# Expert stage written out tile by tile, its bias added outside TensorE, weights loaded in pairs one after another, and half of the residual rows kept on chip

## The chip, the cores and the metric

The kernel runs on one core of one Trainium2 chip. The metric is the device time of one execution in microseconds (us). The core has five engines that each run their own instruction list: TensorE (PE, with its weight loads shown apart as PEld), VectorE (DVE), ScalarE (ACT), GpSimd (POOL) and SyncE (SP, which here only starts transfers). They meet through semaphores. Sixteen DMA engines move data between DRAM and the on-chip memory (SBUF).

## What is computed

One layer over 6250 rows of 256 numbers. A graph part sums weighted neighbour rows, runs a two-layer perceptron and a linear attention; its result is `x`. Then comes the part that the change touches, a mixture of 16 experts of which each row picks two:

```
gate_logits = x @ gate_w + gate_b                 # x here: layernorm of the layer's x
topk_vals, topk_idx = top_k(gate_logits, 2);  topk_w = softmax(topk_vals)
h          = relu(einsum('bsh,ehf->bsef', x, w1) + b1)       # 256 -> 512, per expert
expert_out = einsum('bsef,efh->bseh', h, w2) + b2            # 512 -> 256, per expert
moe = sum(topk_w[..., None] * take(expert_out, topk_idx), axis=2)
y   = x + moe
out = layer_x + layernorm(y) * gamma + beta
```

All of it is in 32-bit floats. The two weights `topk_w` of a row add up to one, so `x + sum(w * e)` is the same as `sum(w * (x + e))`.

## The kernel before, in words

The program is a chain of blocks; between two blocks all engines meet. Rows are handled in 49 tiles of 128.

1. Edges are sorted by row (0 to about 460 us).
2. The graph stage (about 460 to 1618 us): GpSimd gathers 858 sets of neighbour rows, TensorE sums them, and between these units the 49 tiles pass through perceptron, second layernorm and gate. ScalarE's `keep` (L1251 to L1261) stores a tile's normalised row `xn2` to DRAM, copies it into the SBUF array `xh`, and stores the residual row plus beta (`x2b`) to DRAM. Early in the stage VectorE splits the biases `b1` and `b2` (512 + 256 numbers for 16 experts) into three bf16 parts, `bias_split` (L1553 to L1565).
3. A short block (1618 to 1641 us) turns the choices into a list: XT = 114 tiles of up to 128 rows, each with one expert, experts in ascending order. It also starts the load of expert 0's weights.
4. The expert stage (1641 to 2165 us) works on one tile t after another, as a software pipeline. Each engine has a function `step`, run in a hardware loop of two tiles per round by `run_steps`:
   - GpSimd gathers the 128 rows of tile t+4 from DRAM into `tok` (2 buffers, L1884) and scatters the finished rows of tile t-1 to DRAM (L1876). Both read their row numbers from a one-column buffer that GpSimd fills by a copy first (L1864, L1870).
   - TensorE does the first products of tile t (`hidden sums`, 8 products of 128x128 that the profile counts as 16 halves, L1905), the turn of tile t+2 (2 transposes, L1915), then reads tile t-1's expert number into a register (L1919), adds the second bias by a bf16 product of `pick` and `bias_split` (L1923), and does the second products (4 products of 128x256, 8 halves, L1926).
   - ScalarE copies the tile's w1 block next to the others (L1943) after SyncE has counted the expert's weights as landed (`s_wready`, L1849), and copies the turned rows (L1949).
   - VectorE does bias and ReLU (4 instructions, L1962), builds `pick` (L1965) and copies the result to `yrow` (L1971).
   - SyncE has up to four experts' weights in flight (two loads of 512 KB each, L1719 and L1720).
5. The last stage (2166 to 2251 us): per tile TensorE mixes the two expert rows with their weights by diagonal matrices (L2025, L2026) on top of an identity product with `xh` that adds the normalised row (L2023). VectorE computes statistics (L2079, L2084), centres and scales (L2090), and adds the residual row (L2098). SyncE loads expert rows (256 KB per tile) and residual rows (128 KB per tile) and stores the output (128 KB per tile).

Sets of tiles in stage 5 are called groups: 18 of them, of 1 to 4 tiles.

## Time and profile before

| | us |
|---|---|
| median of 3 runs (2249.81 to 2251.22) | 2251.18 |
| the profiled execution, its own time | 2252.68 |
| its span, from first to last instruction | 2250.9 |
| PE busy over the span | 1678.2 (75%) |
| DVE busy | 1377.9 (61%) |
| POOL busy | 1328.5 (59%) |
| expert stage, first gather to last scatter begun | 1642.26 to 2162.66 |
| last stage, first load issued to last store issued | 2166.27 to 2246.65 |

The profile splits the span into instructions with start, duration, and the idle time before each with what ended it. In the rows below a source line (L1905) is a line of the kernel before; `x16` merges consecutive instructions; `[0.68 <-DMA ...]` says that the engine sat idle for 0.68 us until that transfer landed; `<-issue` is idle time in which the engine's own instruction list was late. [...] PEldq is TensorE's own instruction reader.

### The profile page before, as it was taken

The numbers are of one execution on the slowest core, as the hardware profiler recorded it, in microseconds if no ns is written. First come the engines' busy times: TensorE is split into PE (matmuls) and PEld (weight loads), VectorE is DVE, ScalarE is ACT, GpSimd is POOL, SyncE is SP. The second block draws the span as 40 slices with busy tenths as digits, with TensorE's granted clock in tenths as the row PEclk, the third lists the DMA queues.
The fourth block names the chain that finished last, engine by engine and source line by source line (L and its number), as shares of the span: only waits on it lengthen the run. The fifth ranks groups of instructions, "written<-read, shape, count | busy, mean of one in ns | idle before, by whom it ended". The sixth has DMA issues, their size and how long they took to land. (4 is left out here: it accounts for less than half of the span.)

```text
span 2250.9 us, 40865 instructions
## 1 busy us (share of the span) xinstructions
PE 1678.2 (75%) x9702; PEld 1414.8 (63%) x9703; DVE 1377.9 (61%) x4034; ACT 764.5 (34%) x2288; POOL 1328.5 (59%) x1455
## 2 busy tenths in 40 slices
PE   6007888237777787888777887776569999999987
PEld 4007877236655666676666665555458888888876
DVE  4999888368776666666666666564433444334348
ACT  5718889100001323323323222221223333333333
POOL 0007888378777777777777777776024555555510
PEclk9558999668878999889999889997789999999999
DMA  5001011354434444444444444448373111111257
GB/s 162 0 0 36 20 36 36 4 164 131 123 105 121 131 127 126 133 127 127 132 127 126 130 122 126 119 126 91 55 262 104 61 62 59 61 61 61 59 201 279
DMA packets 133895, 232.71 MB, mean 103 GB/s; under 512 B 28854, under 2 KB 85784, under 8 KB 133767
## 3 DMA queue, kind: packets, MB, share of 16 engines
q0 software_dynamic: 56096, 144.39, 23.6%
q1 hardware_dynamic: 49975, 60.99, 8.6%
q10 hardware_dynamic: 27696, 25.83, 3.6%
q8 instruction: 55, 0.90, 0.2%
q14 instruction: 73, 0.60, 0.1%
HBM read 188.69 MB, written 42.43 MB: 103 GB/s over the span
## 5 line engine op out<-in xcount | busy, mean ns | idle before, releaser
L1309 POOL DMA_INDIRECT lower<-xn_rows,lower x858 | 851.1, 992 | 270.1 <-issue 234.6
L1334 PE MATMUL bank<-lower 128*128 x960 | 351.0, 451 | 216.4 <-SPq L1183 175.1
L1334 PEld LDWEIGHTS bank<-lower 128*128 128x128 f32 x960 | 172.9, 213 | 300.7 <-issue 290.1
L1472 DVE TENSOR_TENSOR xh<-xh,bank 128x256 f32 x480 | 200.0, 417 | 242.6 <-PE bank L1335 240.9
L1455 DVE TENSOR_SCALAR lower<-iota_n,lower 128x128 f32<-128x128 f32 x960 | 295.4, 361 | 76.0 <-issue 54.5
L606 POOL DMA_INDIRECT edge_records_sorted<-lower x112 | 204.7, 1828 | 209.0 <-ACT lower L755 179.7
L1335 PE MATMUL bank<-lower 128*128 x960 | 322.9, 421 | 0.0
L683 PE MATMUL bank<-lower 128*64 128x128 f32 x1568 | 192.0, 287 | 113.2 <-ACT lower L739 108.8
L683 PEld LDWEIGHTS bank<-lower 128*64 128x64 f32 x1568 | 185.8, 146 | 116.9 <-DVE lower L942 109.4
L1876 POOL DMA_INDIRECT expert_rows<-arena,dest_idx x114 | 114.6, 1005 | 215.4 <-DVE arena L1971 202.9
L1962 DVE TENSOR_SCALAR arena<-bank,b_tile 128x128 f32<-128x128 f32 x456 | 128.3, 344 | 173.5 <-PE bank L1905 173.5
L1335 PEld LDWEIGHTS bank<-lower 128*128 128x128 f32 x960 | 207.2, 216 | 36.8
L1905 PEld LDWEIGHTS bank<-arena 128*128 128x128 f32 x1824 | 224.1, 194 | 9.0 <-issue 3.0
L1926 PE MATMUL bank<-upper,arena 128*128 x912 | 229.0, 395 | 0.0
L1905 PE MATMUL bank<-arena 128*128 128x128 f32 x1824 | 224.6, 277 | 2.6 <-ACT arena L1943 2.6
L1926 PEld LDWEIGHTS bank<-upper,arena 128*128 128x128 f32 x912 | 167.4, 193 | 30.8 <-issue 5.1
L739 ACT ACTIVATE lower<-lower 128x32 f32<-128x32 f32 x784 | 169.3, 309 | 7.4 <-DVE lower L927 6.6
L1250 ACT ACTIVATE std<-mv,eps_col 128x1 f32<-128x1 f32 x49 | 14.4, 295 | 420.8 <-DVE mv L1622 420.8
L1943 ACT ACTIVATE arena<-lower 128x1024 f32 x114 | 120.5, 1057 | 66.6 <-issue 57.8
L1971 DVE COPY arena<-bank 128x256 f32<-128x256 f32 x114 | 48.4, 425 | 150.1 <-PE bank L1926 150.1
L1949 ACT ACTIVATE arena<-bank 128x256 f32<-128x256 f32 x114 | 43.8, 384 | 284.2 <-PE bank L1915 284.2
L1884 POOL DMA_INDIRECT arena<-xn_rows,tok_idx x114 | 109.4, 960 | 40.1 <-issue 32.5
(337 smaller groups left out, 2531.0 us busy)
## 6 DMA issues: line engine op xcount, KB each, us to landing
lower<-xn_rows,lower POOLq DMA_INDIRECT x858
lower<-in_L_ffn_w SPq DMA_DIRECT2D x16, 512.0 KB, 9.0
upper<-in_L_ffn_w SPq DMA_DIRECT2D x16, 512.0 KB, 10.5
xn_rows<-xh SPq DMA_DIRECT2D x7, 896.0 KB, 4.2
lower<-xn_rows ACTq DMA_DIRECT2D x49, 128.0 KB
xn_rows<-lower ACTq DMA_DIRECT2D x49, 128.0 KB
x_plus_beta<-lower ACTq DMA_DIRECT2D x49, 128.0 KB
upper<-in_x SPq DMA_DIRECT2D x1, 6144.0 KB
```

Source lines behind the costliest of these rows:

```text
L606: pool.indirect_dma_start(rec_dram, bass.IndirectOffsetOnAxis(quad_idx[i][:, c:c + 1], 0), quads[i][:, c * QW:(c + 1) * QW], None).then_in ...
L683: mm = pe.matmul(bank[6 + p][0:NQ * QW, 0:P], moving[p][:, e].rearrange("p c w -> p (c w)"), row_hot[p][:, e, :], start=e == 0, stop=e == ...
L739: done = act.activation(moving[p][:, e, :, 1], col_hot[p][:, e, :], ACT.Copy, scale=group_wgt[p][:, e:e + 1])
L1309: pool.indirect_dma_start(edge_rows[:, t % ROUND, :], None, xn_dram, bass.IndirectOffsetOnAxis(source.bitcast(U32)[:, t:t + 1], 0)).then_i ...
L1334: pe.matmul(sums_at(u), edge_sel[:, 2 * u % ESEL, :], rows_flat[:, ds(at, D)], start=True, stop=False)
L1335: pe.matmul(sums_at(u), edge_sel[:, (2 * u + 1) % ESEL, :], rows_flat[:, ds(at + D, D)], start=False, stop=True).then_inc(s_sum, 1)
L1455: dve.tensor_scalar(edge_sel[:, (2 * u + h) % ESEL, :], iota_n[:], lane[:, at:at + 1], weight_s[:, at:at + 1], ALU.is_equal, ALU.mult).the ...
L1472: dve.tensor_tensor(xh[:, at], xh[:, at], sums_at(u), ALU.add).then_inc(s_acc, 1)
L1905: mm = pe.matmul(bank[2 + p][:, m * P:(m + 1) * P], w1_tile[p][:, c * F + m * P:c * F + (m + 1) * P], tokT[p][:, c * P:(c + 1) * P], start ...
L1926: mm = pe.matmul(bank[6 + p][:, 0:D], hidT[p][:, m * P:(m + 1) * P], upper[:, ds(e * (FC * D) + m * D, D)], start=False, stop=m == FC - 1)
L1943: act.activation(w1_tile[p], lower[:, ds(e * (DC * F), DC * F)], ACT.Copy).then_inc(s_w1t, 1)
L1962: dve.tensor_scalar(hidT[p][:, m * P:(m + 1) * P], bank[2 + p][:, m * P:(m + 1) * P], b1_tile[:, ds(t + m * XT, 1)], 0.0, ALU.add, ALU.max ...
```

## The change

- **Bias.** `b2` is loaded once in plain form to all 128 partitions (`b2_all`, 2 MB, in block 3). VectorE adds gathered row and `b2` of the tile's expert into `yrow` (`biased`, three tiles ahead), and later adds TensorE's result to it (`finish`). So an expert row carries the normalised row too, and the product L1923, its `pick` and the identity product L2023 go. `bias_split` shrinks from 768 to 512 columns.
- **Order.** TensorE, VectorE and GpSimd have the 114 tiles written out one by one; ScalarE keeps its loop. Row numbers are used from `rows_idx` and `dest_idx` directly, without GpSimd copies. `tok` has 4 buffers, `yrow` 6; gathers run 6 tiles ahead.
- **Weights.** From expert 1 on, each 512 KB load waits until the one before has landed; the first waits for the third gather.
- **Residual rows.** `xh` now receives `x2b` instead of `xn2`; the last stage takes the first KEEP = 25 tiles from there and loads only the other 24. The rest of `xh` holds `b2_all` and `yrow`.

TensorE, expert stage, one tile before (`bank` is PSUM, `arena` holds rows, turned rows, hidden rows and the w1 copy, `upper` the w2 weights; names in brackets are the semaphores waited on):

```order
L1905 MATMUL bank<-arena 128x128 [waits expert_hidden,tile_w1_copied,rows_transpose_copied]
L1905 MATMUL bank<-arena 128x128 x7
L1915 MATMUL bank<-ident,arena 128x128 [waits rows_transpose_copied,rows_landed1]
L1915 MATMUL bank<-ident,arena 128x128
L1919 TENSOR_LOAD expert_row
L1919 ISA x2
L1923 MATMUL bank<-bias_split,arena 128x256 [waits expert_rows,bias_pick]
L1926 ISA [waits expert_hidden]
L1926 MATMUL bank<-upper,arena 128x256
L1926 ISA
L1926 MATMUL bank<-upper,arena 128x256
```

and the same tile after:

```order
L1893 MATMUL bank<-arena 128x128 [waits expert_hidden,tile_w1_copied,rows_transpose_copied]
L1893 MATMUL bank<-arena 128x128 x7
L1903 MATMUL bank<-ident,arena 128x128 [waits rows_transpose_copied,rows_landed1]
L1903 MATMUL bank<-ident,arena 128x128
L1912 ISA [waits expert_hidden,expert_rows]
L1912 MATMUL bank<-upper,arena 128x256
L1912 ISA
L1912 MATMUL bank<-upper,arena 128x256
L1880 TENSOR_LOAD expert_row
L1912 ISA
L1912 MATMUL bank<-upper,arena 128x256
```

The register load has moved from behind the turn of the rows to the middle of the second products, for the next tile, and the bias product is gone.

GpSimd, start of the expert stage, before (`row_index_staged` and `result_index_staged` are its own copies of row numbers):

```order
L1870 CAST tok_idx<-rows_all 128x1 [waits rows_landed0]
L1884 DMA arena<-xn_rows,tok_idx 128x256 [waits row_index_staged0,rows_transposed]
L1864 CAST dest_idx<-arena 128x1
L1870 CAST tok_idx<-rows_all 128x1 [waits rows_landed1]
L1876 DMA expert_rows<-arena,dest_idx 27137x256 [waits result_index_staged0,expert_rows]
L1884 DMA arena<-xn_rows,tok_idx 128x256 [waits row_index_staged1,rows_transposed]
```

and after:

```order
L1858 DMA arena<-xn_rows,rows_idx 128x256 x4
L1858 DMA arena<-xn_rows,rows_idx 128x256 [waits rows_transposed,rows_with_bias] x3
L1864 DMA expert_rows<-xh,dest_idx 27137x256 [waits expert_rows]
L1858 DMA arena<-xn_rows,rows_idx 128x256 [waits rows_transposed,rows_with_bias]
L1864 DMA expert_rows<-xh,dest_idx 27137x256 [waits expert_rows]
```

Four gathers go out at once and seven stand ahead of the first scatter.

SyncE, expert weights, before:

```order
L1719 DMA lower<-in_L_ffn_w 128x2x512 [waits weights_of_expert0,rows_landed1]
L1720 DMA upper<-in_L_ffn_w 128x4x256
L1719 DMA lower<-in_L_ffn_w 128x2x512
L1720 DMA upper<-in_L_ffn_w 128x4x256
L1719 DMA lower<-in_L_ffn_w 128x2x512
```

and after:

```order
L1845 DMA lower<-in_L_ffn_w 128x2x512 [waits expert_weights_loaded,rows_landed2]
L1847 DMA upper<-in_L_ffn_w 128x4x256 [waits expert_weights_loaded]
L1845 DMA lower<-in_L_ffn_w 128x2x512 [waits expert_weights_loaded]
L1847 DMA upper<-in_L_ffn_w 128x4x256 [waits expert_weights_loaded]
L1845 DMA lower<-in_L_ffn_w 128x2x512 [waits expert_weights_loaded]
```

Every load now stands behind the landing of the one before it.

The diff, cut to its core:

```diff
-        bias_f = xn_rows[0:96, 0:F + D]
+        bias_f = xn_rows[0:96, 0:F]
...
+        TOKB, YB = 4, 6
+        KEEP = 25
+        carve = carver(xh[:, KEEP * D:NT * D], (NT - KEEP) * D)
+        b2_all = carve(NX * D)
+        yrow = [carve(D) for _ in range(YB)]
...
                     at = ds(bucket_now[s] * D, D)
-                    act.activation(xh[:, at], xn2[s % XB], ACT.Copy).then_inc(s_xn2k, 1)
                     act.dma_start(xn2_dram[ds(bucket_now[s] * P, P), :], xn2[s % XB]).then_inc(s_xn2st, 16)
                     act.wait_ge(s_x2b, s + 1)
                     act.dma_start(x2b_dram[:, at], x2b).then_inc(s_x2st, 16)
+                    act.activation(xh[:, at], x2b, ACT.Copy).then_inc(s_x2k, 1)
...
                 sp.dma_start(gamma_row, row(gamma)).then_inc(s_gamma, 16)
+                sp.dma_start(b2_all, row(b2.rearrange("e d -> (e d)"))).then_inc(s_b2, 16)
...
+                sp.wait_ge(s_we, 32)
+                sp.sem_inc(s_wready, 1)
+                sp.wait_ge(s_tok[2], 16)
+                for e in range(1, NX):
+                    sp.dma_start(w1_sb[:, e], w1[e].rearrange("(c p) f -> p c f", p=P)).then_inc(s_we, 16)
+                    sp.wait_ge(s_we, 32 * e + 16)
+                    sp.dma_start(w2_sb[:, e], w2[e].rearrange("(m p) d -> p m d", p=P)).then_inc(s_we, 16)
+                    sp.wait_ge(s_we, 32 * e + 32)
                     sp.sem_inc(s_wready, 1)
...
+                def gather(t):
+                    if t >= TOKB:
+                        pool.wait_ge(s_tT, t - TOKB + 1)
+                        pool.wait_ge(s_yb, t - TOKB + 1)
+                    pool.indirect_dma_start(tok[t % TOKB], None, xn2_dram, ...rows_idx[:, t:t + 1]...)
+                def scatter(t):
+                    pool.wait_ge(s_yr, t + 1)
+                    pool.indirect_dma_start(y_dram, ...dest_idx[:, t:t + 1]..., yrow[t % YB], None)
+                for t in range(-AHEAD, XT):
+                    if t + AHEAD < XT:
+                        gather(t + AHEAD)
+                    if t >= 0:
+                        scatter(t)
...
+                for t in range(-2, XT + 1):          # TensorE
+                    if 0 <= t < XT:
+                        hidden(t)
+                    if t + 2 < XT:
+                        turn(t + 2)
+                    if t >= 1:
+                        second(t - 1)
...
+                def biased(t):                       # VectorE
+                    e = dve.value_load(expert_row[0:1, t:t + 1], min_val=0, max_val=NX - 1)
+                    dve.wait_ge(s_tok[t % TOKB], t // TOKB * 16 + 16)
+                    if t >= YB:
+                        dve.wait_ge(s_yst[t % YB], t // YB * 16)
+                    dve.tensor_tensor(yrow[t % YB], tok[t % TOKB], b2_all[:, ds(e * D, D)], ALU.add).then_inc(s_yb, 1)
+                def finish(t):
+                    dve.wait_ge(s_y, t + 1)
+                    dve.wait_ge(s_yb, t + 1)
+                    dve.tensor_tensor(yrow[t % YB], yrow[t % YB], bank[6 + t % 2][:, 0:D], ALU.add).then_inc(s_yr, 1)
...
-                        pe.matmul(mixed, ident[:], xh[:, t * D:(t + 1) * D], start=True, stop=False)
                         pe.wait_ge(s_fdiag, TOPK * (t + 1))
-                        pe.matmul(mixed, diag[t % NDG * TOPK], first_row(t), start=False, stop=False)
+                        pe.matmul(mixed, diag[t % NDG * TOPK], first_row(t), start=True, stop=False)
...
+                    if i in OFF:                     # groups from tile 25 on
+                        x2_of = x2_rows[o % XBUF]
+                    else:
+                        x2_of = xh[:, t0 * D:(t0 + m) * D]
```

## Rows read from the trace of the kernel before

**Rows 1.** Busy time by stretch of the expert stage: PE, PEld, DVE, ACT, POOL, clock, DMA
```profile
1645.00:1700.00 55.00, 40.06 (x212) 34.59 (x213) 12.82 (x46) 14.10 (x20) 17.97 (x33) 0.81 0.94 324
1700.00:2155.00 455.00, 430.87 (x2832) 382.09 (x2831) 181.70 (x629) 149.86 (x208) 235.84 (x414) 1.00 0.19 60
```

**Rows 2.** Timeline of two tiles 13 us apart, TensorE: start, us, instruction, idle before
```profile
2101.30 1.95 PE L1905 MATMUL bank<-arena 128*128 128x128 f32 x16
2103.08 0.38 PE L1915 MATMUL bank<-ident,arena 128*128 128x128 f32 x2
2103.30 0.27 PE L1923 MATMUL bank<-bias_split,arena 96*128 96x256 bf16 x1
2103.41 1.89 PE L1926 MATMUL bank<-upper,arena 128*128 x8
...
2105.14 1.95 PE L1905 MATMUL bank<-arena 128*128 128x128 f32 x16
...
2114.58 1.95 PE L1905 MATMUL bank<-arena 128*128 128x128 f32 x16
...
2117.13 0.44 PE L1915 MATMUL bank<-ident,arena 128*128 128x128 f32 x2 [0.60 <-DMA arena<-xn_rows,tok_idx]
...
2117.95 0.28 PE L1923 MATMUL bank<-bias_split,arena 96*128 96x256 bf16 x1 [0.39 <-issue]
...
2120.00 1.95 PE L1905 MATMUL bank<-arena 128*128 128x128 f32 x16
```

**Rows 3.** Waits from 1700 to 2150: us in total, times, longest
```profile
PEld bank L1923 <- issue: 31.2, 61, 0.6
```

**Rows 4.** TensorE's register load (L1919): ns min/median/max, first and last start
```profile
L1919 PEldq TENSOR_LOAD <-expert_row x114: 297/302/320, 1656.7 to 2156.6; - x114
```

**Rows 5.** Timeline, start of the expert stage
```profile
1642.26 0.97 POOL L1884 DMA_INDIRECT arena<-xn_rows,tok_idx  x1 [0.82 <-POOL tok_idx L1870]
...
1645.17 0.66 PE L1915 MATMUL bank<-ident,arena 128*128 128x128 f32 x2 [7.69 <-DMA arena<-xn_rows,tok_idx]
...
1653.68 1.06 ACT L1943 ACTIVATE arena<-lower 128x1024 f32 x1 [4.84 <-SPq L1849]
...
1657.31 1.06 ACT L1943 ACTIVATE arena<-lower 128x1024 f32 x1 [2.29 <-SPq L1849]
...
1660.47 1.95 PE L1905 MATMUL bank<-arena 128*128 128x128 f32 x16
```

**Rows 6.** Time from issue to landing: w1 and w2 of expert 0, alone; then all w1
```profile
DMA to landing us min/median/max: 4.4/4.4/4.4
...
DMA to landing us min/median/max: 3.8/3.8/3.8
...
lower<-in_L_ffn_w SPq DMA_DIRECT2D x16, 512.0 KB, 9.0
```

**Rows 7.** VectorE's bias and ReLU: busy us, mean ns, idle before
```profile
L1962 DVE TENSOR_SCALAR arena<-bank,b_tile 128x128 f32<-128x128 f32 x456 | 128.3, 344 | 173.5 <-PE bank L1905 173.5
```

**Rows 8.** Timeline, end of the expert stage
```profile
2155.63 1.95 PE L1905 MATMUL bank<-arena 128*128 128x128 f32 x16
...
2162.66 0.98 POOL L1876 DMA_INDIRECT expert_rows<-arena,dest_idx  x1 [0.82 <-POOL dest_idx L1864]
```

**Rows 9.** Last stage: a stretch by engine (columns as Rows 1), waits as Rows 3
```profile
2191.31:2230.32 39.01, 38.71 (x171) 31.55 (x170) 36.34 (x124) 20.57 (x63) 0.00 (x0) 1.00 1.00 371
...
DVE stats L2079 <- PE bank L2026: 18.6, 16, 10.5
```

**Rows 10.** Timeline, last stage
```profile
2172.18 0.43 DVE L2079 BATCH_NORM_STATS2 stats<-bank 128x6 f32<-128x256 f32 x1 [10.46 <-PE bank L2026]
...
2191.31 0.41 DVE L2084 BATCH_NORM_AGGREGATE mv<-stats 128x2 f32<-128x6 f32 x3
...
2200.98 0.41 DVE L2084 BATCH_NORM_AGGREGATE mv<-stats 128x2 f32<-128x6 f32 x3
```

**Rows 11.** VectorE's bias split in the graph stage (L1556), columns as Rows 4
```profile
L1556 DVE CAST bias_split<-arena x6: 541/550/551, 487.0 to 494.6; 32x768 bf16<-32x768 f32 x6
```

More of the change, by code:

```diff
@@ L360, in gps_layer @@
         hidT = [carve(F) for _ in range(2)]
-        yrow = [carve(D) for _ in range(2)]
-        pick = [carve(P // 2).bitcast(BF16)[0:96, :] for _ in range(2)]
         dest_all = carve(XT)
@@ L1699, in _ @@
                         unit(u)
[L1704 removed]
+        s_we = sem("expert_weights_loaded")
         s_gap = sem("gate_gaps")
@@ new lines, in turn, with second @@
+                def turn(t):
+                    pe.wait_ge(s_tok[t % TOKB], t // TOKB * 16 + 16)
+                    if t >= 2:
+                        pe.wait_ge(s_tTe, t - 1)
+                    for c in range(DC):
+                        mm = pe.transpose(bank[t % 2][:, c * P:(c + 1) * P], tok[t % TOKB][:, c * P:(c + 1) * P], ident[:])
+                    mm.then_inc(s_tT, 1)
+                def second(t):
+                    p = t % 2
+                    if t >= 2:
+                        pe.wait_ge(s_yr, t - 1)
+                    pe.wait_ge(s_hr, t * FC + FC)
+                    for m in range(FC):
+                        mm = pe.matmul(bank[6 + p][:, 0:D], hidT[p][:, m * P:(m + 1) * P],
+                                       upper[:, ds(expert[t] * (FC * D) + m * D, D)], start=m == 0, stop=m == FC - 1)
+                        if m == 1 and t + 1 < XT:
+                            load_expert(t + 1)
+                    mm.then_inc(s_y, 1)
@@ L1973, in _, with hidden @@
-                run_steps(dve, step, *E_STEPS)
+                LETB = 3
+                def hidden(t):
+                    p = t % 2
+                    dve.wait_ge(s_h, t + 1)
+                    if t >= 2:
+                        dve.wait_ge(s_y, t - 1)
+                    for m in range(FC):
+                        dve.tensor_scalar(hidT[p][:, m * P:(m + 1) * P], bank[2 + p][:, m * P:(m + 1) * P],
+                                          b1_tile[:, t + m * XT:t + m * XT + 1], 0.0, ALU.add, ALU.max).then_inc(s_hr, 1)
@@ L1977, in gps_layer @@
+                dve.wait_ge(s_b2, 16)
+                for t in range(-LETB, XT + 1):
+                    if 0 <= t < XT:
+                        hidden(t)
+                    if t + LETB < XT:
+                        biased(t + LETB)
+                    if t >= 1:
+                        finish(t - 1)
         ENDS = {0: ((0, 1), (1, 1), (2, 2), (4, 3)), NG - 1: ((0, 3), (3, 2), (5, 1), (6, 1))}
```

201 lines of the change are left out of this document (66 added, 135 removed).

## The prediction

> **What bounds the kernel now.** I read the profile from the whole to the part: first the busy shares in 40 slices, then busy time by stretch for the two stages that the change touches, then the timeline of a few tiles, then the waits. [...] One tile takes 3.84 us (2101.30 to 2105.14), another close by 5.42 (2114.58 to 2120.00), with the same instructions [rows 2]. The first is TensorE's own pace: 1.78 for the 16 halves of the first products, 0.22 for the turn, 0.11 for the bias product, 1.73 for the second products. The second is the same with a wait for the gathered rows, and behind it 0.82 between the turn (2117.13) and the bias product (2117.95) instead of 0.22. The gap is the register load of 0.30 us [rows 4], with its register work, that stands behind the turn in TensorE's list: where the rows are early, the reader is ahead of the array and the load costs nothing; where they come just in time, the reader has been held at the turn and the load is exposed. It is exposed at 61 of the some 100 tiles between 1700 and 2150 [rows 3]. From the third tile's first products (1660.47) to the last tile's (2155.63) are 495.16 us for 111 tiles [rows 5, 8]: 4.46 each, 0.62 above the pace. So the stage is bound by late rows and by the weights' start, not by arithmetic.
>
> In its first 55 us the clock averages 0.81 and DMA is 94% busy with weights [rows 1]; the row gathers queue behind them, and only 8 tiles are done (212 matmuls at 27 a tile).
>
> In the last stage TensorE is busy 38.71 of 39.01 us, VectorE 36.34, and DMA is full [rows 9]. Seven tiles take 9.67 us (2191.31 to 2200.98) [rows 10]. VectorE waits for TensorE 16 times for 18.6 us, 10.5 of that before the first tile [rows 9]: TensorE is the bound, with VectorE close behind.
>
> **The change part by part**, counted in the profiled execution (2252.68 us, span 2250.9; the median of the runs is 1.5 below it).
>
> *Pace of a tile.* The bias product goes: 3.84 - 0.11 = 3.73 us. The rows: a gather now stands six tiles ahead of the scatter of its step, and four buffers let it go as soon as the tile four before it has been turned and biased. Its data is needed about three and a half tiles, 13 us, after its issue. A gather in the loaded first stretch would have to take more than that to be late. The load of the expert number now stands between the second and third of four products, for the tile after. The reader has 0.43 us of array work per product in front of it and is no longer held at the turn, so I take its cost as nothing; if the cover fails it is between the load's 0.30 [rows 4] and the whole gap's 0.60 (0.82 - 0.22) [rows 2] on each tile, 33 to 67 us in all. ScalarE's copies and loop stay; it is busy 150 of 455 us [rows 1]. GpSimd drops its two copies and keeps two issues of about 1 us. VectorE has four ReLUs of 0.34 us, loses the pick, gains one add and turns its copy into another; for an add of twice their width I take 0.45, a bit above [rows 7]: 2.3 us, and 2.6 with a register load that nothing covers, under 3.73. `finish` stands behind `biased` in VectorE's list, and the scatter behind `finish`; the row that `biased` waits for was gathered three tiles before. 111 x 3.73 = 414.0. I add 2 for a stretch at 1.2 GHz when the third tile begins after an idle TensorE, and 4 for stray waits: 420.0 against 495.16, **-75.2**. Ends: 414 (no stray, -81) and 4.33 a tile (3.73 + 0.60, 481, -14).
>
> *Start of the stage.* The reference's own gate on the given inputs, counted, gives tiles per expert 1, 1, 41, 1, 18, 14, 1, 0, 2, 1, 1, 4, 12, 0, 8, and the spare tiles last. So tile 1 needs expert 1 and tile 2 expert 2; the trace agrees: ScalarE's copies at 1653.68 and 1657.31 waited for weights [rows 5]. After the change expert 2 is behind four loads in series. The first gather starts at about 1641.25 instead of 1642.26, since the copy and its 0.82 wait are gone [rows 5]; the third begins 2.5 later (two issues of 0.97 and the gaps) and lands 2.9 after that, as the first did (1642.26 to 1645.17), 1646.7. A load on its own took 4.4 and 3.8 us [rows 6], so expert 2 is there at 1646.7 + 2 x 8.2 = 1663.1, and with the copy of 1.06 the third tile starts at 1664.4 instead of 1660.47: **+3.9**. Lower end: the loads take 3.8 each, +2; upper end: they take the 9.0 of loads that share the queues [rows 6], +23. Expert 3 is first needed at tile 43, some 150 us later, and all fifteen pairs take 123 us, so nothing waits after that. The 2 MB of `b2_all` go in ahead of expert 0's w1 at 1618, in a block in which DMA is idle; at the 371 GB/s of [rows 9] it is 6 us, and w1 has 23 until the stage begins: no cost.
>
> *End of the stage.* The last scatter loses GpSimd's copy and the wait of 0.82 for it [rows 8]; with the copy's own 0.2: **-1.0**.
>
> *Last stage.* The identity product is a third of TensorE's work: six halves at 0.216 (1.73 / 8 in [rows 2]) are 1.29 us a tile, four are 0.86. VectorE is next: 9.67 us for seven tiles less its waits in them (0.6) is 9.07, 1.30 a tile. The 8.1 us of waits after the first tile go. The first tile comes 0.9 earlier, two halves at half the clock [rows 9, 10]. Against it, the first tiles at 1.2 GHz need 4 x 0.43 = 1.7 us each on TensorE, more than VectorE's 1.3: I give back 1.5. **-7.5.** The traffic falls from 49 x 512 KB by 25 x 128 KB, 25.7 to 22.4 MB, so DMA, full now, does not take TensorE's place. Ends: -9 (all waits go), and +10 if TensorE stays at half its clock throughout: 49 x 1.71 = 84 us against the 74.5 from the first statistics at 2172.18 [rows 10] to the last store.
>
> [...]
>
> *Graph stage.* The bias split runs from 487.0 to 495.2 on VectorE (the last cast at 494.6 and its 0.55), each step waiting for the one before, 8.2 us [rows 11]. Its width falls to two thirds: 0 to -2.7. VectorE is what holds the heads behind it, and the gathers are not yet at their own pace there, so I take **-2.0**. The copy into `xh` has the same size and only changes place in ScalarE's list; VectorE's new wait for it comes a whole tile later: nothing.
>
> Sum: -75.2 + 3.9 - 1.0 - 7.5 - 2.0 = -81.8. From 2252.68 that is 2170.9, and at the level of the median **2169.5 us**.
>
> **Rivals.**
> 1. *The register load stays exposed*, or rows are still only just in time: about 0.4 a tile, 111 x 0.4 = 44, less the 4 of stray: 2210. For it: 61 exposed loads. Against: in the tile at 2101.30 the same load cost nothing, 3.84. 8%.
> 2. *Serial weights land as slowly as shared ones*, 9.0 each instead of 4.1: third tile at 1683 to 1686, +19 to +23: about 2190. For it: gathers and scatters still share the queues. Against: the solo loads of [rows 6]. 6%.
> 3. *The last stage loses its clock*, as above: up to +17.5 on my sum, 2187; half of that, 2178, is likelier. 10%.
> 4. *Slower than before: the clock of the expert stage.* If TensorE is granted the mean 0.81 of the first stretch [rows 1] through the stage, a tile takes 3.73 / 0.81 = 4.60 and 111 take 511: +16 + 3.9 - 1.0 - 7.5 - 2.0 = +9, 2260. It decides from a mean clock under 0.84. For it: 0.81 with a TensorE that is held up. Against: 1.00 over the 455 us behind it, with more gaps than there will be. 3%.
>
> **How the numbers follow.** My forecast has 73%, with its own range 2162 to 2178. What a measurement of this kernel can tell from no change is about 0.2%, 4.5 us. Every case but the last is faster by more. The fourth holds the chance of slower, and 2% lie in between, where rivals 1 and 2 would meet: faster 0.95, same 0.02, slower 0.03. For eight in ten the range takes in rivals 2 and 3 and leaves out the first: 2160 to 2190.
>
> **What would show it.** Right: first products of consecutive tiles 3.73 apart, no idle time at the turn, third tile at about 1662 (1664.4 less the graph stage's 2), copy waits on weights at tiles 1 and 2 only, DMA share about 0.4 for 130 us, last stage paced by VectorE at 9.1 us for seven tiles. Wrong: tiles that alternate as before; a clock under 0.95 in the last stage; an idle gap between second and third of the second products; ScalarE waiting for weights beyond tile 2.

## The result and the profile after

| | before | after |
|---|---|---|
| median of 4 runs | 2250.49 us (2248.23 to 2251.22) | 2163.53 us (2162.59 to 2167.23) |
| ratio, 95% interval | | 0.9618 [0.9602, 0.9635] |
| profiled execution, span | 2252.68, 2250.9 us | 2162.62, 2160.9 us |
| mean granted clock (1.00 is full speed) | 0.886 | 0.884 |

The forecast was 2169.5 us, in a range of 2160 to 2190; the time is 6.0 below the forecast. The span went down by 90.0 us, the medians by 87.0. The two spans divide at four places that both timelines have; "tile 2" is the third tile, counted from 0:

| stretch | before | after | difference | predicted |
|---|---|---|---|---|
| start to the end of the sort (first gather of the graph stage) | 449.3 | 446.3 | -3.0 | 0 |
| from there to the first gather of the expert stage | 1193.0 | 1191.6 | -1.4 | -3.0 |
| first gather to tile 2's first products | 18.2 | 21.9 | +3.7 | +4.9 |
| 111 tiles, tile 2 to the last | 495.2 | 414.1 | -81.1 | -75.2 |
| last tile to the last stage's first load | 10.6 | 11.6 | +1.0 | -1.0 |
| last stage, first load to the end | 84.6 | 75.4 | -9.2 | -7.5 |

The predicted +4.9 is the +3.9 of the text with the 1.0 by which the first gather was to come earlier; that 1.0 stands in the row above it, with the graph stage's -2.0. The first row is no effect of the change: in the kernels below that ran at the same speed, the sort ended at 448.0 to 454.6.

The busy time by stretch of the changed kernel's expert stage (columns as in [rows 1]: PE, PEld, DVE, ACT, POOL, granted clock, DMA share, GB/s):

```profile
1645.00:1700.00 55.00, 48.49 (x321) 45.45 (x321) 23.02 (x75) 18.39 (x26) 21.92 (x24) 0.90 0.60 188
1700.00:2080.00 380.00, 379.27 (x2636) 357.73 (x2634) 190.48 (x608) 143.65 (x199) 194.33 (x199) 1.00 0.30 92
```

Read it against [rows 1]: in the first 55 us 321 matmuls instead of 212 (301 when the window is laid at the same distance behind the first gather, which came 4.4 us earlier here), with DMA 60% busy and not 94; behind it TensorE has 0.7 us idle in 380, where it had 24 in 455. The timeline of TensorE there, and the time of the register load:

```profile
1700.92 1.95 PE L1893 MATMUL bank<-arena 128*128 128x128 f32 x16
1702.71 0.38 PE L1903 MATMUL bank<-ident,arena 128*128 128x128 f32 x2
1702.93 1.89 PE L1912 MATMUL bank<-upper,arena 128*128 x8
1704.65 1.95 PE L1893 MATMUL bank<-arena 128*128 128x128 f32 x16
...
1708.39 1.95 PE L1893 MATMUL bank<-arena 128*128 128x128 f32 x16
```
```profile
L1880 PEldq TENSOR_LOAD <-expert_row x114: 295/301/714, 1637.2 to 2074.1; - x114
```

1700.92, 1704.65, 1708.39: 3.73 us each, and the rows of one tile follow each other with no idle time in brackets. This is the first of the two tiles of [rows 2] less its bias product, all the way to the end. The load (0.30 us, as in [rows 4]) is done 114 times and shows nowhere as idle time.

The start of the stage, for POOL, ScalarE, SyncE and TensorE (columns as in [rows 5]):

```profile
1637.89 0.95 POOL L1858 DMA_INDIRECT arena<-xn_rows,rows_idx  x1 [23.15 <-POOLq L1718]
...
1650.84 1.06 ACT L1939 ACTIVATE arena<-lower 128x1024 f32 x1 [7.04 <-SPq L1849]
...
1658.64 1.06 ACT L1939 ACTIVATE arena<-lower 128x1024 f32 x1 [6.47 <-SPq L1849]
```
```profile
1643.06 0.37 SPq L1845 DMA_DIRECT2D lower<-in_L_ffn_w  x1
1646.77 0.37 SPq L1847 DMA_DIRECT2D upper<-in_L_ffn_w  x1
1650.78 0.37 SPq L1845 DMA_DIRECT2D lower<-in_L_ffn_w  x1
1654.63 0.37 SPq L1847 DMA_DIRECT2D upper<-in_L_ffn_w  x1
1658.58 0.37 SPq L1845 DMA_DIRECT2D lower<-in_L_ffn_w  x1
```
```profile
1643.51 3.75 PE L1893 MATMUL bank<-arena 128*128 128x128 f32 x16
...
1652.04 3.65 PE L1893 MATMUL bank<-arena 128*128 128x128 f32 x16 [4.35 <-ACT arena L1939]
...
1659.80 2.02 PE L1893 MATMUL bank<-arena 128*128 128x128 f32 x16 [2.16 <-issue]
```

Each load is issued when the one before it has landed, 3.7 to 4.0 us apart; ScalarE's two copies start at the very end of the second and the fourth of them (1650.84, 1658.64), and TensorE starts tiles 1 and 2 behind those copies. Only three other copies wait for weights, by 0.4 to 0.7 us each, and no product waits for them.

The end of the stage, before and after: GpSimd's drain, the instruction with which it closes the stage behind its last scatter.

```profile
L1844 POOLq DRAIN  x1: 706/706/706, 2165.3 to 2165.3; - x1
```
```profile
2073.87 1.95 PE L1893 MATMUL bank<-arena 128*128 128x128 f32 x16
...
2080.55 0.95 POOL L1864 DMA_INDIRECT expert_rows<-xh,dest_idx  x1 [0.77 <-DVE xh L1972]
```
```profile
L1838 POOLq DRAIN  x1: 2009/2009/2009, 2083.2 to 2083.2; - x1
```

The last scatter stands 6.68 us behind the last tile's first products instead of 7.03, but the drain behind it takes 2009 ns where it took 706.

The last stage, 40 us of it, then VectorE's only waits of note in the stage, then seven tiles of it:

```profile
2100.90:2140.90 40.00, 29.58 (x126) 22.83 (x125) 39.68 (x139) 23.26 (x71) 0.00 (x0) 1.00 1.01 368
```
```profile
DVE stats L2087 <- PE bank L2035: 12.1, 4, 10.7
```
```profile
2110.15 1.24 DVE L2098 SCALAR_TENSOR_TENSOR upper<-bank,mv,arena 128x256 f32<-128x256 f32 x3
...
2119.03 1.24 DVE L2098 SCALAR_TENSOR_TENSOR upper<-bank,mv,arena 128x256 f32<-128x256 f32 x3
```

Against [rows 9]: TensorE is busy 29.6 of 40 us instead of 38.7 of 39, VectorE 39.7 instead of 36.3, the clock still 1.00. Of the 18.6 us that VectorE waited for TensorE, only the 10.7 before the first tile are left with 1.4 behind them. Seven tiles take 8.88 us (2110.15 to 2119.03), where they took 9.67.

### The profile page after: what moved, and what is told of

It reads as the page before. It is cut to its first block and busy times, and to the rows that moved or that the text cites. A ratio compares the mean times of both kernels' runs of the same rounds, so it can differ in the third digit from the quotient of the medians.

```text
span 2160.9 us, 38464 instructions
## 1 busy us (share of the span) xinstructions
PE 1603.4 (74%) x9490; PEld 1379.4 (64%) x9490; DVE 1391.8 (64%) x4033; ACT 768.0 (36%) x2288; POOL 1286.3 (60%) x1227
## 5 line engine op out<-in xcount | busy, mean ns | idle before, releaser
L1864 POOL DMA_INDIRECT expert_rows<-xh,dest_idx x114 | 112.1, 983 | 183.4 <-DVE xh L1972 169.1
L1912 PE MATMUL bank<-upper,arena 128*128 x912 | 215.6, 379 | 0.0
L1858 POOL DMA_INDIRECT arena<-xn_rows,rows_idx x114 | 110.7, 971 | 60.5 <-issue 33.5
L941 DVE TENSOR_TENSOR lower<-upper,iota_n 128x3584 f32<-128x3584 f32 (+1 forms) x28 | 108.7, 3883 | 0.0
```

The lines of the kernel that those rows point to most:

```text
L1912: mm = pe.matmul(bank[6 + p][:, 0:D], hidT[p][:, m * P:(m + 1) * P], upper[:, ds(expert[t] * (FC * D) + m * D, D)], start=m == 0, stop=m = ...
```

## The experiments

Twelve kernels ran, in three groups of four, e1 to e4, e5 to e8 and e9 to e12, each on one chip. The chips of the first and of the third group are slower, nearly all of it in one place, in each of the eight kernels profiled there: from the sort to the first gather of the expert stage they take 1409 to 1431 us, where the others take 1192 to 1198 (last section); the sort itself ends 1 to 22 us later. Before was not profiled on these chips; its runs there take 2478 to 2502 us. Each ratio is against before on the same chip. The expert stage is read from its first gather to the last tile's first products, "G" below, and the last stage from its first load to the end, "L". Both hold over the chips: the changed kernel has G 436.0 and L 75.4 in its first profile and 437.6 and 75.7 on such a chip (e12). Before: G 513.4, L 84.6.

| kernel | G us | tile 2 behind first gather | steady median a tile | L us | ratio to before |
|---|---|---|---|---|---|
| before | 513.4 | 18.2 | 4.27 | 84.6 | 1 |
| changed | 436.0 | 21.9 | 3.73 | 75.4 | 0.9618 |
| e1 weights abreast | 433.8 | 17.9 | 3.73 | 76.2 | 0.9649 |
| e2 two row buffers | 687.9 | 21.1 | 5.79 | 75.8 | 1.0630 |
| e3 load behind turn | 436.9 | 21.8 | 3.73 | 75.9 | 0.9653 |
| e4 both | 693.8 | 21.6 | 5.78 | 76.2 | 1.0658 |
| e5 before, paced | 517.5 | 21.8 | 4.30 | 84.3 | 1.0001 |
| e6 two buffers, add last | 476.6 | 21.8 | 3.88 | 75.3 | 0.9802 |
| e7 four buffers, near | 688.5 | 22.1 | 5.79 | 75.5 | 1.0709 |
| e8 wide bias split | 436.1 | 22.1 | 3.73 | 75.5 | 0.9605 |
| e9 all rows loaded | 437.4 | 21.8 | 3.73 | 78.2 | 0.9670 |
| e10 rows and identity | 437.3 | 21.7 | 3.73 | 84.5 | 0.9702 |
| e11 weights early | 429.9 | 14.2 | 3.73 | 76.2 | 0.9601 |
| e12 changed again | 437.6 | 21.9 | 3.73 | 75.7 | 0.9660 |

The theory at the start was the prediction's: the stage was bound by rows that came late, because of the weights in the queues at first and two row buffers throughout, with a register load exposed behind them. The rivals: the load's place in the list, and the order of GpSimd's and VectorE's lists.

**e1: the weights four experts abreast again**

```diff
...
+                for e in range(1, WAHEAD):
+                    load_weights(e)
+                load_weights(WAHEAD)
                 for e in range(1, NX):
-                    sp.dma_start(w1_sb[:, e], ...).then_inc(s_we, 16)
-                    sp.wait_ge(s_we, 32 * e + 16)
-                    sp.dma_start(w2_sb[:, e], ...).then_inc(s_we, 16)
-                    sp.wait_ge(s_we, 32 * e + 32)
+                    sp.wait_ge(s_wr[e % WAHEAD], ...)
                     sp.sem_inc(s_wready, 1)
+                    if e + WAHEAD < NX:
+                        load_weights(e + WAHEAD)
```

> The changed kernel, but the weights of the experts again in groups of four in flight, as before the change. Pacing theory (as in the prediction: the start of the stage is set by what shares the queues with the first gathers): experts 1 to 4 then land together, some 35 us after the third gather; each of the eight loads takes 9 us or more, the clock of the first 55 us falls from 0.90 to about 0.8, expert 2 is there no earlier than in the changed kernel, and the four-row lookahead keeps the gathers early all the same: third tile within 3 us of 1659.8, pace behind 1700 unchanged at 3.73, stage 3 to 25 us longer, 2166 to 2188. Rival (the lookahead alone does everything; pacing delays expert 2 and is worth nothing or less): third tile 1 to 4 us earlier and the same pace: 2159 to 2163.

Measured: ratio 0.9649 [0.9626, 0.9672], beside e3 (the changed kernel with one thing changed that cost nothing) at 0.9653 on the same chip. Tile 2 starts 17.9 us behind the first gather and not 21.9, the pace is 3.73, G is 433.8. The first products of the first three tiles:

```profile
1888.28 3.75 PE L1899 MATMUL bank<-arena 128*128 128x128 f32 x16
...
1895.17 2.66 PE L1899 MATMUL bank<-arena 128*128 128x128 f32 x16 [2.71 <-ACT arena L1945]
...
1900.64 1.95 PE L1899 MATMUL bank<-arena 128*128 128x128 f32 x16
```

The rival was right. With the rows asked for three tiles ahead of the bias add it does not matter that DMA is 98% busy with weights in the 55 us from 1890: from tile 2's first products to tile 8's it takes 22.4 us, where it took 39.5 before. VectorE's bias add does wait there, 11.8 us in all, for earlier scatters to land, but nothing of it reaches TensorE. In the trace pacing the weights costs 2 to 4 us in this kernel and brings nothing; the two ratios do not resolve so little.

**e2: two row buffers, gathers four tiles ahead**

```diff
-        TOKB, YB = 4, 6
+        TOKB, YB = 2, 6
...
-        AHEAD = 6
+        AHEAD = 4
...
-                sp.wait_ge(s_tok[2], 16)
+                sp.wait_ge(s_tok[1], 16)
```

> The changed kernel with two row buffers and four tiles ahead, as before the change (SP's weights start behind the second gather instead of the third). A gather now waits until the tile two before it has been turned and biased. Theory A (the prediction's: the rows of before came late because of the two buffers and their place in the queue): rows are again just in time on part of the tiles, waits on DMA at the turn, 0.2 to 0.6 a tile, 2185 to 2230. Theory B (a row gather lands in 2.6 to 4.6 us and two buffers leave some 7 us, so what mattered was that GpSimd no longer stands behind copies and scatters): pace stays 3.73, 2161 to 2168.

Measured: 1.063 [1.061, 1.0651], slower than before itself, and outside both theories. It takes 5.79 us a tile. One round of it in the trace, without the weight loads and SyncE:

```profile
2099.69 0.98 POOL L1864 DMA_INDIRECT expert_rows<-xh,dest_idx  x1 [3.56 <-DVE xh L1972]
...
2100.98 0.96 POOL L1858 DMA_INDIRECT arena<-xn_rows,rows_idx  x1 [0.31 <-issue]
2103.82 0.20 PEld L1903 LDWEIGHTS bank<-ident,arena 128*128 128x128 f32 x2 [2.03 <-DMA arena<-xn_rows,rows_idx]
...
2103.92 0.42 DVE L1967 TENSOR_TENSOR xh<-arena,xh 128x256 f32<-128x256 f32 x1 [4.03 <-DMA arena<-xn_rows,rows_idx]
...
2104.26 0.41 DVE L1972 TENSOR_TENSOR xh<-xh,bank 128x256 f32<-128x256 f32 x1
...
2105.52 0.98 POOL L1864 DMA_INDIRECT expert_rows<-xh,dest_idx  x1 [3.57 <-DVE xh L1972]
```

One follows from the other, by the releaser that a row names or by its place in the list of its engine: the scatter (0.98, and a gap of 0.31), the gather from 2100.98 to its landing at 2103.92, the bias add L1967 that waited 4.03 us for it, the last add L1972 that stands behind it in VectorE's list, and the scatter, whose issue begins 0.85 behind the end of that. Round to round it is 5.83 us. The ring closes because `biased(t + 3)` waits for rows whose gather stands behind the scatter that `finish`, queued behind `biased`, has to release. That gave a theory with two tests, e6 and e7.

**e3 and e4: the register load behind the turn, with early rows and with late ones**

```diff
                 def second(t):
                     p = t % 2
+                    load_expert(t)
                     ...
-                        if m == 1 and t + 1 < XT:
-                            load_expert(t + 1)
```

> The changed kernel, only with the register load of the expert number taken from between the second products of the tile before and put behind the turn, where it was before the change; the rows stay early. Theory A (the prediction's: the load is exposed only where TensorE's reader is held up at the turn by late rows): with early rows it costs nothing, pace 3.73, 2162 to 2167. Theory B (the load's place is what matters; it is exposed on any tile behind the turn): 0.3 to 0.6 a tile on all 111, 33 to 67 us, 2196 to 2230.

Measured: 0.9653 [0.9629, 0.9676], G 436.9, pace 3.73. Theory A: with early rows the load costs nothing in its old place either. Moving it was not needed. In e4 this edit and that of e2 are made together.

> Two row buffers with four tiles ahead, and the register load behind the turn: both of the last two at once. If late rows and the load's place only cost together (theory A of both), the pace goes back to about 4.2 to 4.4 a tile with waits on DMA at the turn and a gap behind it, 2215 to 2240, more than the two single costs added. If they are independent, the cost is the sum of the two single ones.

Measured: 1.0658 [1.0633, 1.0683], G 693.8 against 687.9 in e2. With late rows the load does show, as in [rows 3]; the first row is e4's from 1950 to 2500, the second a tile of it:

```profile
PEld bank L1913 <- issue: 32.5, 91, 0.4
```
```profile
2105.78 1.59 PEld L1913 LDWEIGHTS bank<-upper,arena 128*128 128x128 f32 x8 [0.36 <-issue]
```

0.36 us at 91 of the tiles, and yet the steady pace is 5.78 as in e2: TensorE is not in the ring, so idle time in front of it costs nothing there. I had expected a pace of 4.2 to 4.4 and the two to cost clearly more together than added. Neither came: G grows by 252 in e2, by 1 in e3 and by 258 in e4, one profile each, and the intervals of e2 and e4 overlap, so the 5 between are not settled.

**e5: before, with paced weights**

```diff
...
+                for e in range(1, NX):
+                    sp.dma_start(w1_sb[:, e], ...).then_inc(s_we[0], 16)
+                    sp.wait_ge(s_we[0], 32 * e + 16)
+                    sp.dma_start(w2_sb[:, e], ...).then_inc(s_we[0], 16)
+                    sp.wait_ge(s_we[0], 32 * e + 32)
                     sp.sem_inc(s_wready, 1)
-                    if e == 0:
-                        sp.wait_ge(s_tok[1], 16)
-                        for later in range(1, WAHEAD):
-                            load_weights(sp, later)
-                    if e + WAHEAD < NX:
-                        load_weights(sp, e + WAHEAD)
```

> The kernel before the change, only with the experts' weights loaded one transfer at a time, as in the changed kernel. With the lookahead of the changed kernel pacing the weights cost 3.9 us at the third tile and gave nothing back. Theory A (before the change the late rows of the first 55 us were late because of the weights in the queues, the prediction's reading): here pacing gives back part of the first stretch, 8 tiles in 55 us become 10 to 12, 10 to 20 us faster over the stage, less 4 at the third tile. Theory B (the rows are late by the order of GpSimd's list, whatever else is in the queues): the pace stays at 4.4 to 4.5 a tile from the first tiles on, and the kernel is the same or up to 4 us slower.

Measured: 1.0001 [0.9987, 1.0016]. This kernel's first gather is at 1649.42, 7.2 us behind that of before, so the stretch to lay beside the first of [rows 1] is the one at the same distance from it:

```profile
1652.16:1707.16 55.00, 44.77 (x263) 39.33 (x264) 16.23 (x58) 16.74 (x24) 22.22 (x41) 0.87 0.55 171
```

That is 263 matmuls and not 212, some ten tiles and not eight. The time from issue to landing of a row gather says why; before from 1640 to 1700, before from 1700 on, and e5 from 1649 to 1707:

```profile
DMA to landing us min/median/max: 2.8/5.6/6.2
```
```profile
DMA to landing us min/median/max: 2.7/2.8/3.6
```
```profile
DMA to landing us min/median/max: 2.7/3.1/3.6
```

With four experts' weights in flight a gather took up to 6.2 us, and from tile 2 to tile 8 it was 39.5 us; paced, a gather took at most 3.6 in this stretch, and the six tiles 27.0. So theory A was right on what made the rows late in the first 55 us. It was wrong on the whole: tile 2 comes 3.6 us later, and the 8.9 us that e5 is ahead at tile 8 are gone by tile 24 (127.3 us behind the first gather, before 126.0). The paced weights are still being loaded until some 120 us, where before has issued its last load at 47, and in that time two of e5's tiles take 7.5 and 7.6 us. The 111 tiles take 495.7 us, against 495.2. Theory B has the rest: behind tile 24 both kernels need some 4.4 us a tile, before with no weights left to load. What holds the rows there is not the weights, and e5 doesn't show what it is.

**e6: two buffers, but the last add ahead of the bias add**

```diff
...
+                    if t >= 1:
+                        finish(t - 1)
                     if t + LETB < XT:
                         biased(t + LETB)
-                    if t >= 1:
-                        finish(t - 1)
```

The edit of e2 is in it too.

> Two row buffers and four tiles ahead, as in the kernel that took 5.8 us a tile, but in VectorE's list the last add of a tile stands ahead of the bias add that waits for a later tile's rows. Ring theory (from the trace of that kernel: gather issue and landing 3.9, bias add and last add 0.8, scatter issue and gap 1.3 follow each other round and round, because the bias add of tile t+3 waits for rows that are gathered behind the scatter of tile t-1, which waits for the add behind it): the ring is broken, pace 3.73 to 3.9. Rival (two buffers are too few in themselves, since a gather waits for the turn and the bias add of the tile two before): pace between 4.5 and 5.8.

Measured: 0.9802 [0.9769, 0.9836]. From e2's 5.8 the pace falls to a median of 3.88, on average 4.10 (454.8 us for 111 tiles): the ring is broken by the order of two instructions, as the ring theory said, though the average is 0.2 above its range. What is left from 1700 to 2100:

```profile
PEld bank L1903 <- DMA arena<-xn_rows,rows_idx: 22.9, 37, 2.5
```

Over the 111 tiles e6 is 40.7 us above the changed kernel, and the row above gives 22.9 of it as TensorE's waits for rows. That is the price of two buffers with four tiles ahead; the two were not parted in this order of the adds.

**e7: four buffers, but gathers only four tiles ahead**

```diff
-        AHEAD = 6
+        AHEAD = 4
```

> Four row buffers as in the changed kernel, but gathers only four tiles ahead of the scatter of their step instead of six; VectorE's list as in the changed kernel. Ring theory: the rows of tile t+4 are issued behind the scatter of tile t-1 and the bias add of tile t+4 stands in front of the last add of tile t, so the ring is there with any number of buffers: 5.6 to 5.8 a tile. Rival (the buffers are what counts): 3.73 a tile.

Measured: 1.0709 [1.0674, 1.0743], G 688.5, the same as e2 with half the buffers. From 1700 to 2300:

```profile
DVE xh L1967 <- DMA arena<-xn_rows,rows_idx: 420.8, 100, 6.5
...
POOL expert_rows L1864 <- DVE xh L1972: 353.5, 95, 5.2
```

VectorE waits 4.2 us for rows at each of 100 tiles, and GpSimd 3.7 for VectorE. In this order of VectorE's list four buffers are worth nothing without the two tiles more of lookahead.

**e8: the bias split at its old width**

```diff
-        bias_f = xn_rows[0:96, 0:F]
-        bias_r = xn_rows[0:96, F:2 * F]
+        bias_f = xn_rows[0:96, 0:F + D]
+        bias_r = xn_rows[0:96, F + D:2 * (F + D)]
...
```

> The changed kernel with the bias split of the graph stage at its old width of 768 instead of 512 columns (the extra 256 are loaded and split, and not used). If the narrower split is what brought 1.8 us on VectorE there: the split takes 8.2 us again (6.45 in the changed kernel). By the prediction 2.0 of it reach the end of the graph stage. Rival: they are lost in the wait of the heads for gathered rows, and nothing before the expert stage moves by more than runs of one kernel differ.

Measured: 0.9605 [0.9573, 0.9637]. The split takes 8.5 us (489.97 to 498.45) and 6.5 in the changed kernel. From the sort's end to the first gather: 1196.2, beside 1194.6 and 1195.3 in e6 and e7, which have the narrow split and ran on the same chip. e5, with the wide split of before and on the same chip too, takes 1198.3, of which 1.0 may be its later first gather. So 1 to 3 us of the split may reach the end of the graph stage, but these are single profiles, and those of one width differ by 0.7 and 1.1 themselves; it stays inconclusive.

**e9 and e10: the last stage's loads, and the identity product**

```diff
-        OFF = [i for i, (t0, _, _) in enumerate(GROUPS) if t0 >= KEEP]
+        OFF = list(range(len(GROUPS)))
```
```diff
+                        pe.matmul(mixed, ident[:], xh[:, t * D:(t + 1) * D], start=True, stop=True)
                         pe.wait_ge(s_fdiag, TOPK * (t + 1))
```

The first edit is in both, the second in e10 only.

> The changed kernel, but in the last stage the residual rows of all 49 tiles are loaded again from DRAM instead of 24; no identity product. It is the last stage that is asked: from SyncE's first load there to the end were 84.6 us before and 75.4 in the changed kernel. Theory A (the prediction's: TensorE was the bound and the identity product's end is the gain): the stage stays within 1.5 us of 75.4, since the 25.7 MB of before need 69 us at the 371 GB/s that it reached. Rival (DMA was full before, and the 3.3 MB less are the gain): 82 to 85 us.

> As the one before (all residual rows loaded again), and with the identity product back on TensorE as extra work: its result is overwritten by the next product, so the output doesn't use it. Theory A: this brings the old last stage back, 83 to 86 us, with VectorE waiting for TensorE 15 to 19 us in its steady part. Rival (TensorE was not the bound, the loads are): same as the one before.

Measured: L 78.2 in e9 (ratio 0.9670 [0.9638, 0.9701]) and 84.5 in e10 (0.9702 [0.9661, 0.9743]); 75.7 in e12 on the same chip, 84.6 before. e10 first, then e9, 40 us of the stage each:

```profile
2344.10:2384.10 40.00, 39.35 (x174) 31.93 (x172) 36.98 (x125) 21.08 (x65) 0.00 (x0) 1.00 1.00 370
```
```profile
2348.50:2388.50 40.00, 30.02 (x126) 22.57 (x124) 39.68 (x139) 23.21 (x71) 0.00 (x0) 1.00 1.06 403
```

e10 is the last stage of before again: 84.5 us against 84.6, with TensorE as full as in [rows 9]. With the identity product gone (e9) VectorE is the bound, and DMA moves 403 GB/s where it moved 370: it had looked full at a share of 1.00 and was not. VectorE's waits in the stage, e10 and then e9:

```profile
DVE stats L2090 <- PE bank L2036: 20.0, 16, 11.6
```
```profile
DVE upper L2113 <- DMA lower<-x_plus_beta: 1.3, 1, 1.3
```

Behind the first tile VectorE waits 8.4 us for TensorE in e10 (20.0 less 11.6), as the 8.1 of [rows 9], and not the 15 to 19 that the expectation gave. Of the 9 us the identity product is 6.3 (84.5 to 78.2) and the 25 row tiles kept in SBUF are 2.5 (78.2 to 75.7): mostly theory A, with a part for the loads that it put at under 1.5. That part lies at the start and not in the steady run: e9 issues its fourth store 21.2 us behind the first load, where e12 does at 18.8, and from there to the end they take the same time. A wait of VectorE for residual rows, 1.3, is half of it.

**e11 and e12: the weights of experts 1 to 3 in the idle block before, and the changed kernel again**

```diff
                 sp.dma_start(w2_sb[:, 0], ...).then_inc(s_we, 16)
+                for e in range(1, WAHEAD):
+                    sp.dma_start(w1_sb[:, e], ...).then_inc(s_we, 16)
+                    sp.wait_ge(s_lists, TOPK * FC * (e + 1))
+                    sp.dma_start(w2_sb[:, e], ...).then_inc(s_we, 16)
...
-                sp.wait_ge(s_we, 32)
-                sp.sem_inc(s_wready, 1)
-                sp.wait_ge(s_tok[2], 16)
-                for e in range(1, NX):
+                sp.wait_ge(s_we, 32 * WAHEAD)
+                sp.sem_inc(s_wready, WAHEAD)
+                for e in range(WAHEAD, NX):
```

> The changed kernel, with the weights of experts 1 to 3 loaded in the block before the expert stage, in which DMA is nearly idle; experts 4 to 15 stay one at a time. In the changed kernel tiles 1 and 2 start 14.1 and 21.9 us behind the first gather because they wait for weights, and tile 0 at 5.6. Theory A (only weights hold those two tiles): tile 1 at about 9.4, tile 2 at 13 to 14.5, all after it 3.73 apart: 7 to 9 us off the whole, ratio to before about 0.958 where the changed kernel has 0.962. [...]

> The changed kernel itself once more, unaltered, on the chip of the three before, to read them against: stages as in its first profile (tile 2 at 21.9 us behind the first gather, 3.73 a tile, last stage 75.4), ratio 0.960 to 0.9635; the graph stage may differ with the chip.

Measured, on one chip: e11 2386.33 us median (6 runs), ratio 0.9601 [0.9571, 0.9631]; e12 2398.01 (6 runs), 0.9660 [0.9631, 0.9689]. The first gather of e11 is at 1865.21; its first three tiles:

```profile
1871.70 3.75 PE L1896 MATMUL bank<-arena 128*128 128x128 f32 x16 [0.52 <-issue]
...
1875.67 1.97 PE L1896 MATMUL bank<-arena 128*128 128x128 f32 x16
...
1879.42 1.95 PE L1896 MATMUL bank<-arena 128*128 128x128 f32 x16
```

Tile 2 is at 14.2 us and not at 21.9, G is 429.9 and not 437.6: both 7.7 less, theory A (tile 1 comes at 10.5, where it gave 9.4). The first products of tile 0 take 3.75 us at a granted clock of 0.50 (1871.7 to 1875.4), those of tile 1 1.97 at 0.99 (1875.67 to 1877.6). Whole runs give 11.7 between the medians with intervals that just touch, so I trust the 7.7 of the trace. This kernel beats before by 4%, and the changed one by those 7.7 us. e12 has the stages of the first profile, but its ratio of 0.9660 lies above the 0.960 to 0.9635 expected: the 88 us less are a smaller share of the 2486 us that before takes on this chip.

## Why the prediction came out right, step by step

- *What bounds the stage.* "Bound by late rows and by the weights' start, not by arithmetic" held. So did the reason that the text gave for late rows in the first 55 us, "the row gathers queue behind" the weights: their landing took up to 6.2 us there and 2.8 behind it, and e5, which thins the weights out, has at most 3.6 and gets from tile 2 to tile 8 in 27.0 us and not 39.5. What did not hold is the cure: paced weights alone win nothing (e5), and with rows asked for early no pacing is needed (e1).
- *Pace of a tile.* 3.73 was exact (1700.92, 1704.65, 1708.39). 111 tiles took 414.1 us, the lower end of the text; the +2 for the clock and +4 for stray waits were not needed. The runs give the clock as a share of full speed alone, so the 1.2 GHz that the text names with this +2 is shown by none of them. What they show is tile 1's first products at 3.65 us and a granted clock of 0.53 (1652.0 to 1655.7), and tile 2's, after 2.16 us of idle TensorE, at 2.02 and 1.00, with tile 3 following 3.81 behind (1663.61). That the load costs nothing was right. Its new place between the products, by which the text argued, was not what did it: it costs nothing behind the turn too, once the rows are early (e3), as the text had said of the tiles of before with early rows.
- *The sum.* The span fell by 90.0 and not 81.8. Of the 8.2 between, 5.9 are the stray waits and 3.0 are the sort, which the change doesn't touch and which was luck; the start and the last stage gave 1.2 and 1.7 more than forecast, the graph stage and the end 1.6 and 2.0 less. The total is closer than its parts because they partly cancel.
- *What it rests on.* The text took four buffers and six tiles ahead as one step, and wrote of the wait in `biased` only that its row "was gathered three tiles before". That is the condition on which the whole edit hangs, and that six tiles ahead met it was not worked out, so it was in part luck. With four tiles ahead, one tile before, the kernel is 7% slower than before instead of 4% faster (e7), and no rival named it: rival 4 looked for a slower kernel in the clock. The price could be read from the change: 2.9 from a gather's issue to its landing [rows 5], two adds of 0.45 by the text's own estimate and a scatter of 1.0 [rows 8] are 4.8 a tile before any gap, against 3.73.
- *How the 81.1 us divide.* The bias product is 111 x 0.11 = 12.2. Four buffers with six tiles ahead instead of two with four are 40.7 (e6). The last 28.2 us, between before's 495.2 and e6's 454.8 less the bias product, are GpSimd's two copies, the load exposed behind late rows (31.2 us in [rows 3]), the slow gathers of the first 55 us and the new order together; I didn't run them apart. By place, 17.0 of the 81.1 lie in the six tiles from tile 2 to tile 8 (39.5 and 22.5).
- *Start.* Four loads in series took 15.5 us (1643.06 to 1658.58), predicted 16.4. With the sort 3.0 earlier than in the profile of before, 1664.4 - 2.0 - 3.0 = 1659.4 for tile 2; it came at 1659.80. That it is so close is chance: the first gather came 1.6 later than forecast and the loads landed 0.9 sooner. Rival 2, weights at 9.0 each, didn't happen.
- *End of the stage.* -1.0 was wrong by 2.0. The wait of 0.82 for GpSimd's copy went, but one of 0.77 for the last add stands in its place, so that the last scatter came 0.35 sooner and not 1.0; and the drain took 1.3 more, which no row of before could have shown.
- *Last stage.* -7.5 against -9.2. The mechanism is shown: put the identity product back and the old stage is back (e10). Seven tiles took 8.88 and not 9.07. The first statistics stand 4.9 us behind the first load and not 5.9, as forecast, and the 1.5 given back for the slow first tiles is not seen. No run shows a clock of 1.2 GHz for these either. From one product of two halves to the next it is 0.85 us at a granted clock of 0.50, in the first tiles of before (2170.13 to 2170.98) and of the changed kernel (2090.05 to 2090.90), and in 0.43 at 1.00 (2093.08 to 2093.51). "DMA is full" was a misreading: e9 moved 403 GB/s with the same transfers. The clock is 0.50 in the first 6.5 us of the stage and 1.00 from 2092.5 to 2145, so rival 3 didn't happen: TensorE idle a quarter of the time (29.58 of 40) kept its full clock. That pauses of this kind could cost it the clock was an assumption of the text that no run showed.
- *Graph stage.* -2.0 for the split: 1.7 us less on VectorE (6.5 against 8.2), of which the whole path shows 0.4 here (-1.4 with the 1.0 of the first gather) and 1 to 3 in e8. Not settled, and within what the stage varies.

## What to carry to other kernels

When a consumer is moved ahead in an in-order list (here the bias add three tiles ahead of its tile), count how many steps before it its gather was issued, and ask whether anything queued behind the consumer releases that gather: if so it is a ring, and its round trip divided by those steps is the least time of a tile, whatever the number of buffers. Here the round trip was 5.83 us: over one step it set the pace (e2, e7); over the changed kernel's three it would be 1.9 by this estimate, under TensorE's 3.73; two steps (five tiles ahead) were not run. Look ahead far enough first; with early rows the place of the register load cost nothing (e3) and that of the bulk weight loads 2 to 4 us (e1). Weights that the first tiles need belong in a block in which DMA is mostly idle (a share of 0.38 over the 23 us ahead of the changed kernel's first gather), not in a careful order behind the first rows: that gave 7.7 us (e11).

## What the runs showed of the hardware

- GpSimd's drain at the end of the expert block took exactly 706 ns in both kernels with before's GpSimd list (before and e5) and 2009 ns in the changed kernel and in the eleven runs made from it, whatever their pace. Why is not known: the changed list is unrolled and reads its indices from one tile, and neither was tried alone.
- A DMA share of 1.00 is no proof of a bound: 371 GB/s at 1.00 in [rows 9], 403 GB/s at 1.06 in e9, with the same transfers.
- A gather of 128 rows takes from issue to landing 2.8 us (median) at a DMA share of 0.19, with no weights left to load, and up to 6.2 at 0.94, with four experts' weights in flight (before, from 1700 on and before it). With one load of 512 KB at a time it stayed under 4 us in e5 and at 4.6 or less in the changed kernel, in the gathers whose landing the trace has.
- Two of the chips took 210 us or more longer between the sort and the expert stage in every kernel profiled there, with the changed kernel's expert stage and last stage equal within 1.6 us. What GpSimd's row gathers wait for is SyncE's line L1177, which is no transfer: SyncE does more in this stage than start transfers, it counts up a semaphore there once TensorE has summed a set of rows, and lets the next gathers go. The changed kernel on the one chip and on the other, in that order:

```profile
SPq L1177: 35.9, 88
```
```profile
SPq L1177: 235.1, 125
```

SyncE itself waits at different places, in the same order:

```profile
SPq L1182 <- DMA lower<-xn_rows,lower: 907.1, 428, 10.4
```
```profile
SPq L1177 <- PE bank L1334: 383.0, 128, 9.1
```

On the first chip it waits for gathers to land, on the other first of all for TensorE's sums. Why these come late there is open; no run was made to find out. One kernel can so take 11% longer on another chip, and a stage has to be read from a mark of its own.
